# The softmax denominator's constant added by ScalarE instead of VectorE

## The reference

```python
s = jnp.einsum('bhid,bhjd->bhij', q * scale, k)
gm = jax.lax.stop_gradient(jnp.max(s, axis=-1, keepdims=True))
p = jnp.where(causal_mask, 0.0, jnp.exp(s - gm))
num = jnp.einsum('bhij,bhjd->bhid', p, v)
out = num / (jnp.sum(p, axis=-1, keepdims=True) + EPS)     # EPS = 1e-08
```

## Time and profile before

| | |
|---|---|
| median of 3 runs | 1317.78 us (1317.76 to 1317.88) |
| profiled execution, its time | 1317.02 us |
| its span | 1314.9 us |
| mean granted TensorE clock | 0.988 |
| busy: TensorE, VectorE, ScalarE, POOL | 96%, 83%, 64%, 65% |

### The profile page before, as it was taken

The page is one execution under the profiler, slowest core; times in us unless marked ns, Lnnn a source line. Parts: engine busy times, 40 slices in busy tenths (PEclk is TensorE's granted clock), DMA queues, the critical chain, the costliest instruction groups (busy, mean ns, idle before and its releaser), DMA issues.

```text
span 1314.9 us, 34208 instructions
## 1 busy us (share of the span) xinstructions
PE 1268.4 (96%) x10194; PEld 1031.1 (78%) x10194; DVE 1086.3 (83%) x2557; ACT 838.2 (64%) x2892; POOL 848.3 (65%) x1595
## 2 busy tenths in 40 slices
PE   6899999999999999999999999999999999999984
PEld 4678888878888878878878888878888878888863
DVE  6678888888888888888889888888888888988765
ACT  5766666766666766666766666676666676666640
POOL 5656666676666676666676666676666666666654
PEclk9999999999999999999999999999999999999995
DMA  3000000000000000000000000000000000000000
GB/s 109 17 15 23 18 10 22 18 22 22 16 10 22 18 22 22 16 16 16 18 22 22 16 20 12 18 22 22 19 19 10 22 18 22 20 17 6 19 19 10
DMA packets 38920, 26.53 MB, mean 20 GB/s; under 512 B 2896, under 2 KB 34128, under 8 KB 38896
## 3 DMA queue, kind: packets, MB, share of 16 engines
q1 hardware_dynamic: 38480, 25.96, 6.8%
q10 hardware_dynamic: 416, 0.26, 0.1%
HBM read 21.94 MB, written 4.28 MB: 20 GB/s over the span
## 4 chain that ended last, share of the span: by engine, by line
PE 92%; DVE 3%; POOL 2%; ACT 1%; issue 1%; DMA 0%; DVEq 0%; POOLq 0%
PE ps_m L1029 27%; PE ps_s L1128 18%; PE ps_m L1003 16%; PE ps_o L1158 14%; PE ps_m L1081 9%; PE ps_s L1138 5%; PE ps_m L1105 4%; ACT probs L659 0%; DVE neg_max L858 0%; DVE probs_t L793 0%; DVE xn L782 0%; POOL probs L451 0%; POOL rstd L495 0%; DVE qy L62 0%; DVE h_r L874 0%
## 5 line engine op out<-in xcount | busy, mean ns | idle before, releaser
L659 ACT ACTIVATE probs<-ps_s,neg_max 128x128 f32<-128x128 f32 (+1 forms) x1024 | 424.2, 429 | 391.9 <-PE ps_s L1138 391.9
L451 POOL TENSOR_SCALAR probs<-probs,r_den 128x256 f32<-128x256 f32 (+1 forms) x768 | 346.4, 466 | 0.0
L858 DVE TENSOR_REDUCE neg_max<-ps_s 128x4 f32<-128x1024 f32 x256 | 304.0, 1219 | 7.0 <-PE ps_s L1128 6.9
L1128 PE MATMUL ps_s<-qk 64*128 64x256 f32 x2048 | 258.5, 391 | 0.6 <-ACT qk L617 0.6
L793 DVE COPY probs_t<-ps_m 128x512 f32<-128x512 f32 x256 | 176.6, 690 | 78.4 <-PE ps_m L1003 74.3
L1003 PE MATMUL ps_m<-ident,probs 128*128 128x128 f32 x1536 | 230.8, 273 | 2.8 <-DVE probs_t L793 1.6
L1128 PEld LDWEIGHTS ps_s<-qk 64*128 64x128 f32 x2048 | 185.1, 186 | 47.8 <-issue 12.4
L449 POOL TENSOR_TENSOR probs<-probs,r_den 128x128 f32<-128x128 f32 x256 | 102.6, 401 | 185.6 <-DVE r_den L869 166.7
L659 ACT ACTIVATION_READ_ACCUMULATOR probs<-ps_s,neg_max 128x1 f32 x1024 | 217.3, 212 | 0.0
L73 POOL TENSOR_TENSOR qy<-qy,qm 128x352 f32<-128x352 f32 (+1 forms) x96 | 83.0, 865 | 183.6 <-DVE qm L66 181.2
L1158 PE MATMUL ps_o<-probs_t,v 128*64 128x256 f32 (+1 forms) x2048 | 195.4, 333 | 1.5 <-ACT o_t L649 1.5
(11 more groups left out here) (110 smaller groups left out, 1800.8 us busy)
## 6 DMA issues: line engine op xcount, KB each, us to landing
mod_a<-mod_rows SPq DMA_DIRECT2D x32, 256.0 KB, 3.3
x_res<-L_attn_x SPq DMA_DIRECT2D x32, 128.0 KB, 2.1
out<-y_out SPq DMA_DIRECT2D x32, 128.0 KB, 1.8
x_in<-L_attn_x SPq DMA_DIRECT2D x31, 128.0 KB, 2.1
mod_b<-mod_rows SPq DMA_DIRECT2D x32, 64.0 KB, 2.8
wkv<-L_attn_Wkv SPq DMA_DIRECT2D x3, 256.0 KB, 5.8
wo<-L_attn_Wo SPq DMA_DIRECT2D x1, 512.0 KB, 5.5
wkv<-L_attn_Wkv SPq DMA_DIRECT2D x2, 128.0 KB, 3.1
```

The costliest lines, as they stand in the source:

```text
L451: ins = nc.gpsimd.tensor_scalar(cols, cols, r_den[:, u % 4, s:s + 1], 1.0, ALU.mult, ALU.mult)
L659: ins = nc.scalar.activation(probs[:, u % 4, h, t * P:(1 + 2 * t) * P], ps_s[:, 2 * (u % 2) + h, t * N:t * N + (1 + t) * P], ACT.Exp, bias ...
L858: nc.vector.tensor_reduce(neg_max[:, u % 4, :], ps_s[:, 2 * (u % 2):2 * (u % 2) + 2, :].rearrange("p b (t j) -> p (b t) j", t=2), AX.X, AL ...
L1128: mm = nc.tensor.matmul(ps_s[:, 2 * (u % 2) + h, t * N:(t + 1) * N], qk[rows, u % 4, 0, t * P:(t + 1) * P], qk[rows, u % 4, 1, :], start=( ...
```

## The change

ScalarE adds the constant with an ACTIVATE of the function Identity with the constant as its bias, right behind the second head's exponentials. It first waits for the exponentials' own semaphore, since the sums must have been written. VectorE's addition goes, and its reciprocal waits for ScalarE's new semaphore step. The bias is a new tile of one column that POOL sets at the start, so ScalarE waits for POOL's set-up before its first activation.

```diff
+        soft_eps = sb("soft_eps", [P, 1])
...
-        POOL_SETUP = 7
+        POOL_SETUP = 8
...
             init(nc.gpsimd.memset(ln_eps[:, :], LN_EPS))
+            init(nc.gpsimd.memset(soft_eps[:, :], SOFTMAX_EPS))
...
             act.dma_start(wq[:, QK_CHUNKS[0]], w_q[:, QK_CHUNKS[0]]).then_inc(wq_in[0], 16)
+            act.wait_ge(pool_setup, POOL_SETUP)
             act.wait_ge(cond_in, 16)
...
                         ins.then_inc(exp_done, 1)
+                        if h == 1:
+                            act.wait_ge(exp_done, 16 * i + 2 * u + 2)
+                            nc.scalar.activation(den_eps[:, u % 4, :], den[:, u % 4, :], ACT.Identity,
+                                                 bias=soft_eps[:, 0:1], scale=1.0).then_inc(eps_added, 1)
...
                 def denominators(u):
                     if not has.unit(u):
                         return
-                    dve.wait_ge(exp_done, 16 * i + 2 * u + 2)
-                    nc.vector.tensor_scalar(den_eps[:, u % 4, :], den[:, u % 4, :], SOFTMAX_EPS, None,
-                                            ALU.add).then_inc(eps_added, 1)
                     dve.wait_ge(eps_added, UNITS * i + u + 1)
                     nc.vector.reciprocal(r_den[:, u % 4, :], den_eps[:, u % 4, :]).then_inc(rden_ready, 1)
```

## The result

The changed kernel takes 1347.78 us (median of 4 runs, 1343.85 to 1350.49) against 1317.77 us (1317.66 to 1317.88): ratio 1.0225, 95% interval 1.0198 to 1.0253. Forecast were 1344.8 us and a range of 1326 to 1356. The profiled execution took 1346.30 us with a span of 1344.5.

A forecast was written before the change was run, and what follows sets the result against it. TensorE was taken to bound the kernel, its chain covering 92% of the span. Losses of 0.11 + 0.32 + 0.47 = 0.90 us per period over 30 elements give 27 us: 1317.8 + 27 = 1344.8 us, range 1326 to 1356.

The forecast's parts named there:

- ScalarE's delay: Whatever stands behind the new instruction on ScalarE is late by 0.32 us, bounds 0.24 to 0.40, unless ScalarE would idle there.
- The walk: Following the 0.32 us delay through one batch element's period to TensorE's waits: 0.90 us lost per period; chance 0.72.
- pair 0: Late qk copy delays the xq transposes and gate; v's wait for the second qk copy leaves TensorE losing 0.11 us.
- pair 1: The second gate waits for the qk copy, then tanh, gating and second up projection follow: TensorE loses 0.32 us.
- pairs 2 and 3: Late copies delay hq transposes, unit 7's scores and the down projection; the POOL wait takes back 0.28: 0.47 us lost.
- The relief of VectorE: Removing 256 additions gives VectorE 49 us back; costed at nothing because its work is hidden behind TensorE.
- The reciprocal's new wait: VectorE's reciprocal now waits for ScalarE; operand there at about 602.95, VectorE comes at 603.35: cost nothing.
- the start: ScalarE's first activation waits for POOL's extra memset; up to 1.3 us if the table load comes behind, taken as 0.
- Absorption: Rival: ScalarE's idle time before the masks swallows the delay; all absorbed 1318 us (chance 0.08), half 1324 us (0.12).
- Relief of VectorE as a gain: Rival: 0.19 us saved in units 4 and 5 shortens TensorE's wait for POOL; at most 7.5 us, 1310; chance 0.05.
- A delay above 0.40: Rival: ScalarE's whole sequencer stalls, so the added delay exceeds 0.40 us: beyond 1356 us; chance 0.03.
- The table load: Rival: ScalarE loads a table at each Exp/Identity change, 512 of 1.28 us: beyond 1900 us; no separate chance given.

The follow-up runs named there:

- instruction-alone run: Kernel before, plus a ScalarE instruction of the same form behind head 1 of each unit, without the wait, writing an unread tile: 1330.94 us, ratio 1.0087.
- The two runs by units: Kernel before, VectorE's addition kept, ScalarE's wait and instruction (unread result) only in units 0, 2, 5: 1338.44 us; only in 1, 3, 4, 6, 7: 1324.51 us.
- run with both additions: Changed kernel with VectorE's addition put back; ScalarE's result goes to a tile that nobody reads: 1345.74 us, ratio 1.0210.
- no addition at all: Kernel before without VectorE's addition and nothing on ScalarE; the reciprocal takes the sums themselves: 1314.12 us, ratio 0.9975.
- the run with the wait alone: Kernel before, with ScalarE waiting for its own exponentials behind head 1 of each unit, no new instruction: 1331.70 us, ratio 1.0095.
- the run with VectorE's copies alone: Kernel before, addition on VectorE, with the copy of qk0 in pairs 0 and 1 moved from ScalarE to VectorE: 1316.97 us, ratio 0.9980.
- the one with unit 4's addition beside them: Kernel before with qk0's copy in pairs 0 and 1 on VectorE, and ScalarE adding the constant for unit 4 alone: 1314.47 us, ratio 0.9967.

## Why the prediction was right

**ScalarE's delay.** Mis-sized a little. Forecast were 0.21 + 0.03 + 0.17 - 0.09 = 0.32; measured are 0.21 + 0.04 + 0.20 to 0.21 - 0.09 = 0.36 to 0.37. The term that was short is the time that the instruction holds the engine, 0.17 for 0.20. The straight line through two exponentials gave 0.15. The changed kernel shows 0.20 to 0.21 and the instruction-alone run 0.18 to 0.19. The estimate of 0.19 from the figures of the Trainium skill ("ScalarE: Activation LUTs", "What ACT_TABLE_LOAD costs") agrees with the trace of the latter run. Against the term that was short stands that the copies are 0.03 shorter behind the wait and the new instruction, which I had not foreseen, so that what TensorE sees is 0.33. That this lies so near the forecast 0.32 is in part luck.

**The walk.** Right in every stretch within 0.03 us: pair 0 0.11 against 0.14, pair 1 0.32 against 0.34, pairs 2 and 3 0.47 against 0.50. The two runs by units show that its places are the right ones. Its main steps are seen in the trace: the 0.20 of idle ahead of v used up in pair 0, in pair 2 the 0.15 ahead of the next qk projection gone (no idle at its load, 640.98) and unit 7's scores on the copy of qk, and in pair 3 the wait for POOL taken back and the last down projection waiting.

**The relief of VectorE.** "I cost it at nothing" holds for this change (0.01 us per period between the two runs with and without the addition), and for the reason given: the one wait where it would show is used up. As a statement on VectorE's work by itself it was wrong: without ScalarE's part it is worth 0.13 us per period.

**The reciprocal's new wait, the start.** Cost nothing, as forecast: the first scores start at the same time. The wait becomes real only when the addition is moved later on ScalarE.

**From the period to the total.** 30 elements at 0.90 were to give 27 us. Span against span it is 29.6. The last element's scores start at 1255.42 instead of 1224.85, 30.6 later: 2.5 of it in the first element, 2.9 in the next four, and 26 at 0.97, 25.2. The stretch behind is 1.0 us shorter than before (89.1 and 90.1 us); TensorE's mean granted clock is 0.85 in it and was 0.82, which fits, but no run separates it. "The first two add about nothing" did not hold in these traces, but of the 2.5 us only 0.2 are in the run with both additions, whose clock did not fall in the first element (last section): most of the 2.5 goes with the clock and not with the added instructions.

**Rivals.** Absorption fails: the slack that there is (0.20 ahead of v, 0.15 ahead of qk in pair 2, 0.30 ahead of hq) was already in the sum. Relief of VectorE as a gain fails for this change, though its mechanism is real (no addition at all). A delay above 0.40 did not come (0.36 to 0.37). The table load did not come: the groups by line show one.

## What to carry to other kernels

An operation moved from a busy engine to an idler one costs what it delays behind itself in that engine's queue, not its busy time: of eight places per period three cost 0.70 us and five 0.18. On ScalarE the instruction that needs the accumulator's result delayed the copy behind it by 0.36 us: its own 0.20 and the wait for the read's end. Placed behind the copies that are needed soon, the same pair cost 0.16 us per period and not 1.1 (39.27 and 40.20 against 39.11 with no addition). When the walk shows where an engine's relief can matter, move only that one: one addition of eight, unit 4's, brought 0.11 us per period, where leaving out all eight brought 0.13.

## What was not expected of the hardware

**ScalarE's recorded lengths depend on what stands ahead.** A copy of 512 columns is 0.60 long behind an accumulator's read (median 0.597) and behind the instruction without a wait (0.596), 0.59 behind a bare wait and 0.57 behind wait and new instruction (median 0.566), while the spacing to the next instruction stays at 0.47 to 0.48. So the time from the copy's start to its end, on which TensorE waits, must be read from the trace where the copy stands, and not carried over from another place.

**A register operation behind a wait seems to be in the open.** In the run with the wait alone the copy starts 0.12 behind the end of the read, with a register operation between the two; in the changed kernel the new instruction starts 0.04 behind it. No run varies the register operation by itself.

**The first element and TensorE's clock.** The table of stretches compares a steady period; the first element took 35.1 us before, 37.5 in the changed kernel, and 35.3 in the run with the addition on both engines, which has the same instructions on ScalarE. Two timelines of TensorE, first the changed kernel's, then that run's, ahead of unit 2's scores in the first element:

```profile
20.40 1.47 PE L1033 MATMUL ps_m<-wkv_r,h_r 128*128 128x512 f32 x3 [2.04 <-ACT qk L620]
21.79 1.65 PE L1132 MATMUL ps_s<-qk 64*128 64x256 f32 x6
```

```profile
19.83 0.97 PE L1038 MATMUL ps_m<-wkv_r,h_r 128*128 128x512 f32 x3 [2.06 <-ACT qk L622]
20.73 2.00 PE L1137 MATMUL ps_s<-qk 64*128 64x256 f32 x16
```

The same matmuls take 1.47 us in the one and 0.97 in the other. The windows from 20 to 30 us (length; busy time and count for each engine; granted clock; DMA) show the clock, first the changed kernel, then the other:

```profile
20.00:30.00 10.00, 8.82 (x51) 6.23 (x53) 4.78 (x7) 6.33 (x24) 6.95 (x16) 0.83 0.01 2
```

```profile
20.00:30.00 10.00, 8.69 (x63) 6.26 (x65) 5.33 (x12) 7.11 (x28) 8.87 (x21) 1.00 0.01 2
```

TensorE was granted the lower of its two levels, 1.2 GHz, for a part of the window (mean 0.83) in the one and 2.4 GHz throughout in the other, after idle stretches of nearly the same length (2.04 and 2.06 us). Six of the fourteen profiled programs (both kernels and the twelve experiments) show 0.83 there, and their first elements take 36.05 to 38.49 us. Of the eight with 1.00, the run with VectorE's copies alone and the one with unit 4's addition beside them show 0.83 in the window from 30 to 40 us instead (in the first of the two behind an idle stretch of 2.25 us), and take 36.57 and 36.98; the other six take 33.44 to 35.91. So every first element with such a stretch is longer than every one without. Single times of the changed kernel lie 6.6 us apart with mean clocks of 0.984 to 0.989, the two slower ones at 0.984 and 0.985. What decides the level there is open; it was not tried.
